# Setup and first batches of an adaLN attention + routed experts layer: weights split in two, q,k product signalled by bank

## The reference, cut to what matters

```
mod = silu(c) @ wmod                      # sa, ca, ga, sb, cb, gb: 8 x 128 each
h = layernorm(x) * (1 + ca) + sa
q, k, v = split(rms_norm(h) @ w_qkv.T)    # w_qkv 384 x 128
q, k = rms_norm(q), rms_norm(k)
w  = cumsum(exp(k));  kv = cumsum(exp(k) * v)
y  = sigmoid(q) * kv / (w + 1e-6)
u, g = split(y @ w_swiglu.T)
x = x + ga * (h + (u * silu(g)) @ w_out.T)
...                                       # layernorm, router, dispatch, experts, combine
```

## Time and profile before

| | us |
|---|---|
| median of 3 runs | 222.36 (222.19 to 223.55) |
| the profiled execution | 221.95 |
| its span | 220.2 |
| busy in the span: PE / DVE / ACT / POOL | 186.2 / 153.3 / 150.9 / 101.5 |

### The profile page before, as it was taken

One profiled execution on the slowest core, in us unless ns is written; L12 is line 12 of the kernel. 1 busy time (PEld: TensorE's weight loads), 2 busy tenths in 40 slices (PEclk: granted clock), 3 DMA queues, 4 the chain that ended last, 5 costly groups with the idle time before them and its releaser, 6 DMA issues.

```text
span 220.2 us, 3901 instructions
## 1 busy us (share of the span) xinstructions
PE 186.2 (85%) x1128; PEld 149.4 (68%) x1128; DVE 153.3 (70%) x478; ACT 150.9 (69%) x438; POOL 101.5 (46%) x115
## 2 busy tenths in 40 slices
PE   7979989998998999698657779999999999999300
PEld 5858678687875988666445437788888887887100
DVE  3799799999999899999873244376684774836400
ACT  5398999999999999986562906558576485643000
POOL 6130132442046347656886520007466485474770
PEclk9999999999999999999995599999999999999855
DMA  5999999991104113412552229999977854110010
GB/s 143 290 347 358 360 351 327 335 263 58 48 3 151 47 48 127 158 53 79 183 194 83 78 77 304 358 355 323 322 228 218 287 160 149 33 42 12 24 37 0
DMA packets 37284, 38.60 MB, mean 175 GB/s; under 512 B 2591, under 2 KB 31334, under 8 KB 37264
## 3 DMA queue, kind: packets, MB, share of 16 engines
q1 hardware_dynamic: 33936, 31.29, 45.5%
q0 software_dynamic: 3328, 7.07, 9.0%
HBM read 19.19 MB, written 18.95 MB: 173 GB/s over the span
## 4 chain that ended last, share of the span: by engine, by line
PE 57%; DVE 16%; ACT 11%; issue 7%; POOL 4%; DMA 1%; POOLq 1%; DVEq 0%; ACTq 0%
PE bank L1194 16%; PE bank L1180 13%; PE bank L962 5%; ACT junk L476 3%; ACT ewkv L495 3%; PE bank L1063 2%; PE bank L1158 2%; PE bank L1014 2%; POOL dispatched_rows L417 2%; DVE w1l L882 2%; POOL out_dram L439 2%; PE bank L979 2%; PE bank L1151 2%; PE bank L1031 2%; PE bank L1000 2%
## 5 line engine op out<-in xcount | busy, mean ns | idle before, releaser
L439 POOL DMA_INDIRECT out_dram<-x_all,rest x40 | 42.2, 1054 | 43.4 <-DVE x_all L912 34.0
L417 POOL DMA_INDIRECT dispatched_rows<-rows,slot x32 | 31.5, 985 | 17.0 <-DVE slot L800 8.5
L1194 PE MATMUL bank<-HT,w 128*128 128x320 f32 x128 | 37.0, 432 | 0.0
L637 ACT ACTIVATE HT<-bank 128x320 f32<-128x320 f32 x64 | 28.0, 439 | 9.4 <-PE bank L1180 9.0
L1194 PEld LDWEIGHTS bank<-HT,w 128*128 128x128 f32 x128 | 23.5, 189 | 7.6
L1180 PE MATMUL bank<-xth,w1h 128*128 128x320 f32 x64 | 22.9, 358 | 0.3 <-DVE xtl L888 0.3
L924 DVE COPY OT<-bank 128x320 f32<-128x320 f32 x16 | 7.9, 492 | 21.9 <-PE bank L1194 21.9
L882 DVE TENSOR_TENSOR w1l<-w,w1h 128x1024 fp32r<-128x1024 f32 x8 | 16.2, 2028 | 6.9 <-DMA dispatched_rows<-rows,slot 6.9
L1180 PE MATMUL bank<-xth,w1l 128*128 128x320 f32 x64 | 19.8, 309 | 0.0
L1180 PE MATMUL bank<-xtl,w1h 128*128 128x320 f32 x64 | 19.8, 309 | 0.0
L476 ACT ACTIVATE junk<-bank 128x128 f32<-128x128 f32 x64 | 16.6, 291 | 2.6 <-PE bank L962 2.6
(11 more groups left out here) (161 smaller groups left out, 458.9 us busy)
## 6 DMA issues: line engine op xcount, KB each, us to landing
w<-in_L_ffn_w_dram SPq DMA_DIRECT2D x16, 512.0 KB, 8.3
dispatched_rows<-blank SPq DMA_DIRECT2D x8, 965.0 KB, 12.6
rest<-dispatched_rows SPq DMA_DIRECT2D x8, 645.0 KB, 6.4
hin<-dispatched_rows SPq DMA_DIRECT2D x7, 320.0 KB, 7.7
x_all<-in_L_attn_x_dram SPq DMA_DIRECT2D x8, 256.0 KB, 5.1
rows<-gb_row SPq DMA_DIRECT2D x8, 256.0 KB, 5.9
out_dram<-rows SPq DMA_DIRECT2D x8, 256.0 KB
out_dram<-x_all,rest POOLq DMA_INDIRECT x40, 3.0
```

Source lines behind the costliest of these rows:

```text
L417: pool.indirect_dma_start(out=disp_d, out_offset=bass.IndirectOffsetOnAxis(ap=slot[:, b, j:j + 1], axis=0), in_=rows[:, b, j, :], in_offse ...
L439: pool.indirect_dma_start(out=out_d.rearrange("b t d -> (b t) d"), out_offset=bass.IndirectOffsetOnAxis(ap=rest[i % RING][:, n, C_TOK - D: ...
L637: act.activation(HT[e][:, f, :], ps_h[c % HB][:, 0:CAP], ACT.Gelu_apprx_tanh).then_inc(h_done, 1)
L1194: last = pe.matmul(ps_o[e], w2[i % RING][:, e, f, :], HT[e][:, f, :], start=(f == 0), stop=(f == NF - 1))
```

## The change

Five edits. The transfers of the gate and swiglu weights raise a semaphore of their own, `w_more`. TensorE transposes the q,k,v weights alone, behind c_s, in the place of the last early matmul; the other weights are transposed behind `transpose1(0)`, into `ps_u`, and ScalarE copies them in `keep_more`, behind `ln1_scale(1)`. `modulation_products` comes behind `project_qk(0)`. VectorE does `normalize1(1)` ahead of `modulations`. In the attention, `qk_ps` is raised once per bank of `ps_qk`, and `square_sums` waits bank by bank; `exp_qk` does the four exponentials of k first and raises `ek_done`, for which `weigh_v` and `transpose_k` now wait, then those of q.

```diff
-            sp.dma_start(gw[:, :], gate_w_d).then_inc(w_in, 16)
-            sp.dma_start(wsw[:, :, :], w_swiglu_d.rearrange("(m e) d -> e m d", m=2)).then_inc(w_in, 16)
+            sp.dma_start(gw[:, :], gate_w_d).then_inc(w_more, 16)
+            sp.dma_start(wsw[:, :, :], w_swiglu_d.rearrange("(m e) d -> e m d", m=2)).then_inc(w_more, 16)
...
             def square_sums(b):
-                after(act, qk_ps, b)
                 after(act, nrm_b, b, 1)
                 for j in range(NJ):
+                    if j % 2 == 0:
+                        after(act, qk_ps, 2 * b + j // 2)
...
-                for j in range(NJ):
-                    for m in range(2):
+                for m, done in ((1, ek_done), (0, ew_done)):
+                    for j in range(NJ):
                         last = act.activation(t[:, j, m, :], ps_qk[:, j, m * D:(m + 1) * D], ACT.Exp,
                                               scale=nrr[:, 2 * j + m:2 * j + m + 1])
-                last.then_inc(ew_done, 1)
+                    last.then_inc(done, 1)
...
             def keep_weights():
                 act.wait_ge(wt_ps, 1)
                 act.mul(wqkvT[:, 0:D], bank01[:, 0:D], -1.0)
-                act.copy(wqkvT[:, D:3 * D], bank01[:, D:3 * D])
-                act.copy(wswT[:, :], bank01[:, 512:512 + 2 * D])
-                act.copy(gwT[:, :], bank01[:, 512 + 2 * D:512 + 2 * D + NE]).then_inc(wt_done, 1)
+                act.copy(wqkvT[:, D:3 * D], bank01[:, D:3 * D]).then_inc(wt_done, 1)
+
+            def keep_more():
+                act.wait_ge(wt_ps, 2)
+                act.copy(wswT[:, :], ps_u[:, 0:2 * D])
+                act.copy(gwT[:, :], ps_u[:, 2 * D:2 * D + NE]).then_inc(wt_done, 1)
...
-            ln1_scale(0); keep_weights(); modulate1(0); ln1_scale(1); square_sums(0); modulate1(1)
+            ln1_scale(0); keep_weights(); modulate1(0); ln1_scale(1); keep_more(); square_sums(0); modulate1(1)
...
             def weigh_v(b):
                 after(dve, v_ps, b)
-                after(dve, ew_done, b)
+                after(dve, ek_done, b)
...
-            stats1(1); aggregate1(1); modulations(); normalize1(1); diagonal(0); h_means(0)
+            stats1(1); aggregate1(1); normalize1(1); modulations(); diagonal(0); h_means(0)
...
                     last = pe.matmul(ps_qk[:, j, :], hT[b % NHT][:, j * P:(j + 1) * P], wqkvT[:, 0:2 * D],
                                      start=True, stop=True)
-                last.then_inc(qk_ps, 1)
+                    if j % 2 == 1:
+                        last.then_inc(qk_ps, 1)
...
             def transpose_k(b):
-                after(pe, ew_done, b)
+                after(pe, ek_done, b)
...
             pe.transpose(bank3[:, 0:NB], c_s[:, :], ident[0:NB, 0:NB]).then_inc(mod_ps, 1)
-            run_early(1)
+            pe.wait_ge(w_in, 16)
+            for m in range(3):
+                last = pe.transpose(bank01[:, m * D:(m + 1) * D], wqkv[:, m, :], ident[:, :])
+            last.then_inc(wt_ps, 1)
...
             def weights_over():
-                pe.wait_ge(w_in, 48)
-                for m in range(3):
-                    pe.transpose(bank01[:, m * D:(m + 1) * D], wqkv[:, m, :], ident[:, :])
+                claim(pe, "u", wt_done, 1)
+                pe.wait_ge(w_more, 32)
                 for m in range(2):
-                    pe.transpose(bank01[:, 512 + m * D:512 + (m + 1) * D], wsw[:, m, :], ident[:, :])
-                pe.transpose(bank01[:, 512 + 2 * D:512 + 2 * D + NE], gw[:, :], ident[0:NE, 0:NE]
-                             ).then_inc(wt_ps, 1)
+                    pe.transpose(ps_u[:, m * D:(m + 1) * D], wsw[:, m, :], ident[:, :])
+                pe.transpose(ps_u[:, 2 * D:2 * D + NE], gw[:, :], ident[0:NE, 0:NE]).then_inc(wt_ps, 1)
...
-            weights_over(); transpose1(0); modulation_products(); project_qk(0); h_square_sums(0)
+            transpose1(0); weights_over(); project_qk(0); modulation_products(); h_square_sums(0)
```

More of the change, by code:

```diff
@@ L206, in adaln_attention_moe @@
         c_in, wmod_in, w_in, blank_out = [sem(n) for n in ("c_in", "wmod_in", "w_in", "blank_out")]
-        wmod_rest, wout_in = sem("wmod_rest"), sem("wout_in")
+        wmod_rest, wout_in, w_more = sem("wmod_rest"), sem("wout_in"), sem("w_more")
         mod1_done = sem("mod1_done")
@@ L234, in adaln_attention_moe @@
         pool_past = sem("pool_past")
+        ek_done = sem("ek_done")
         last_sent = sem("last_sent")
```

## The result

The changed kernel took 226.89 us (median of 4 runs, 225.05 to 227.62) against 222.96 for the kernel before beside it (4 runs, 222.19 to 224.40): a ratio of 1.0136 [1.0087, 1.0186]. It is slower; the medians lie 3.9 us, or 1.8 per cent, apart, and 226.89 lies above the range of 220.6 to 224.4. Ratios are formed from the faster executions of each kernel, those within 1.5 per cent of its fastest, and none is given where too few are left. The profiled execution took 227.17, its span 225.4, against 221.95 and 220.2.

The account below looks back on a forecast made before the run. The prediction took VectorE's dense stream from diag_ga to den(0) to set the pace, so TensorE's setup gain would not reach the end. Terms +0.6 - 0.2 + 0 = +0.4 us gave a median of 222.8 us, range 220.6 to 224.4.

Parts of the forecast that it names:

- Setup on TensorE: Setup: q,k,v transposes take 0.7 us, hT(0) is there at 8.1 not 9.35, modulation products end at 10.95 not 9.14.
- Balance at diag_ga: VectorE in setup: later modulation products, +1.80 us, offset by normalize1(1) moved ahead and a shorter 128x8 operation; net -0.05.
- The early hT(1) and its collision: Batch 0: earlier hT(1) releases GpSimd's hsq(1) under diag_ga; it then slows VectorE's qk_means(0), +0.75 us.
- term 1: Setup through den(0) and lden(0): the delay at qk_means(0) passes down the chain, +0.6 us (bounds -0.2 and +0.9).
- Term 2: Attention, batches 1 to 7: signals by bank remove ScalarE's 0.20 us wait before batch 3, -0.2 us.
- Term 3: Attention: exponentials of k first offer transpose_k and weigh_v data sooner, but gain 0 us (bounds -0.5 and 0).
- Moved behind it: the four modulation products, 0.81: Setup: products behind project_qk(0) end 1.8 us later, delaying VectorE's modulation work, in exchange for normalize1(1) moved ahead.
- Rival 3: Setup: dropping an early matmul makes TensorE's clock rise later, slowing transpose1(0) and project_qk(0); +2.3 + 0.4, 225.0 us; chance 0.09.
- slower: Whole kernel: measured time over 224.6 us, mostly from a late clock rise; chance 0.11.

Follow-up runs that it names:

- the early gap filled: Changed kernel with one filler matmul of 256 columns on constants behind the modulation products only; median 229.15 us against 223.52 for the kernel before, no ratio.
- the late one: Changed kernel with two filler matmuls of 320 columns on constants ahead of project_v(0) only; ratio 1.0070 [1.0025, 1.0115] to the kernel before.

## Why the prediction was wrong, step by step

- **Setup on TensorE**: right. The q,k,v transposes took 0.86 (0.7 forecast), hT(0) ended at 8.49 instead of 8.1, nearly all of it the late x. Modulation products: forecast to end at 10.95, ended at 11.32.
- **Balance at diag_ga**: right. Forecast 12.6; 13.00, with x 0.37 late. The 1.03 us operation is a 0.17 one (L832).
- **The early hT(1) and its collision**: right in kind and nearly in size. hsq(1) at 14.12, qk_means(0) 0.71 instead of 0.17: +0.54 where +0.75 was taken. With TensorE held at the upper level the chain then ends where term 1 put it (den(0) done 22.39 for 22.35). The Trainium skill (SBUF — State Buffer, section Who interferes with whom) has a VectorE instruction with two SBUF inputs contend with a GpSimd instruction that reads SBUF, and the order of issue decide which of them blocks. The traces agree: qk_means(0) takes 0.71 us with hsq(1) begun before it and 0.17 without, and hsq(1) itself 1.88 instead of 1.04 with diag_gb begun before it.
- **Term 2, bank signals**: the mechanism and the 0.26 us at batch 3 were right; none of it reaches the end. **Term 3**: 0; the attention edits as a whole moved nothing, and no run parts this term from term 2.
- **The step that failed** is in "Moved behind it: the four modulation products, 0.81". I charged the move to VectorE only and took every TensorE duration behind it from rows at 2.4 GHz: "project_qk(1) starts at 17.8". What the move did to TensorE's own load was not asked: it strings sixteen narrow records together, with a wait of 0.38 us in the middle, where before project_qk(0) lay in between. The granted clock then fell at 13 us, and project_v(0) and the row products, on the way to project_qk(1), cost 0.92 + 1.74 us more. That made 17.8 into 19.8 (+2.0). A second fall, at 74.6 to 78.0 us, lies where the delay grows from +2.7 to +4.0; a third at 98.5 to 101.9 and the longer one at the end of attention lie where the last 1.2 are added. No run takes these later steps apart.
- **Rival 3** had the right resource and the wrong event. It asked whether the clock would rise later, and gave 225.0; its test ("if the products of batch 0 show the early, half pace") came out negative in the profiled run: 1.99 us. Other executions were not so: in six later traces of kernels with the new setup the product took 3.4 to 3.8 us, by a second fall or a late rise, and late rises came in kernels with the old setup too. The rows for the right question stood in front of me: 0.52 at 115.8 to 117.8, behind a lightly used stretch. I used them to price the lower level and not to ask where the change makes another such stretch. The Trainium skill (TensorE: Matmul & The Clock Gate, section HAM oscillation — how this bites in real kernels) tells of a kernel whose waits between groups of matmuls throw it back to the lower clock each time. The traces here agree that a clock once risen falls again in the middle of a kernel, but show it without long waits: none over 0.49 us between the rise and this fall.
- **The chances**: slower had 0.11. A mechanism that the profile shows at one place of this kernel, and that a move can bring to another, deserved its own rival on this side.

What stays open: why the fall near 75 us comes with some delays of the stream and not with others (with the early gap filled it was there, with the late one not, and in the look at the kernel before with its late rise it was there too); what in the stretch ahead of 13 us brings the fall there, since no run changed the narrow matmuls themselves; in how many executions the clock falls at 8, at 13 or not at all; and how much of the 1.1 per cent without the early matmul is real.

## What to carry to other kernels

When a change strings small matmuls together, or thins out TensorE's work, ahead of wide ones, price the wide ones at the lower clock as well; read the PEclk row, not only the waits, and for the time ahead of the first rise the durations of the matmuls. Matmuls on constants in the gaps are cheap to try; here it took them in all the gaps of the setup to keep the clock up. A wait that is not on the path (here 1.8 of ScalarE's 2.6 us, with the attention edits alone) can be removed without moving the end, and the instructions that it frees early can collide elsewhere.

## What was not expected of the hardware

- Useless matmuls made the kernel faster: in the tail 1 per cent off by the ratios, in two measurements, one of them clear of no change, though the medians of all executions hardly moved.
- Executions of one unchanged kernel lie on steps that go with the mean granted clock. On one chip the kernel before took 222.5 to 222.6 us at 0.944 to 0.945, 223.0 to 223.5 at 0.937, and 224.5 to 225.0 at 0.930 to 0.932. Three more executions lie off these steps, 227.7 to 228.2 at 0.931 to 0.938.
- The first rise to 2.4 GHz came at 4.7 to 6.7 us in twelve traces, but at 11 to 21 us in eight, the kernel before among them (14.3, its first q,k product 3.44 us for 1.99).
